# Row sums of the softmax and a one-row mask in a chain of four cross-attention layers

## Time and profile before

| what | value |
|---|---|
| median of 3 runs | 991.19 us (991.05 to 992.46) |
| profiled execution, its own time | 991.19 us |
| its span | 989.4 us |
| TensorE busy | 953.5 us (96%) |
| VectorE busy | 737.7 us (75%) |
| ScalarE busy | 574.4 us (58%) |
| GpSimd busy | 360.8 us (36%) |
| chain that ended last, TensorE's share | 80% |
| chain that ended last, VectorE's share | 8% |

### The profile page before, as it was taken

One profiled execution on the slowest core, in us unless ns is written; L12 is line 12 of the kernel. 1 busy time (PEld: TensorE's weight loads), 2 busy tenths in 40 slices (PEclk: granted clock), 3 DMA queues, 4 the chain that ended last, 5 costly groups with the idle time before them and its releaser, 6 DMA issues.

```text
span 989.4 us, 20036 instructions
## 1 busy us (share of the span) xinstructions
PE 953.5 (96%) x8028; PEld 822.3 (83%) x8028; DVE 737.7 (75%) x1259; ACT 574.4 (58%) x1193; POOL 360.8 (36%) x413
## 2 busy tenths in 40 slices
PE   6999999999998998999999999999999999999997
PEld 5777566556776998998999999999999999889997
DVE  5878999899999788565776677877666766786542
ACT  3557788787876654364545455444544554465552
POOL 2332689898641333011212222431122212282210
PEclk9999999999999999999999999999999999999999
DMA  8302000000000500034233224331222121200001
GB/s 307 106 2 86 1 2 1 2 1 1 2 1 1 204 31 2 1 130 146 74 100 107 84 96 163 108 102 48 86 87 78 51 86 46 83 1 12 23 22 33
DMA packets 31268, 62.30 MB, mean 63 GB/s; under 512 B 4420, under 2 KB 9288, under 8 KB 30536
## 3 DMA queue, kind: packets, MB, share of 16 engines
q1 hardware_dynamic: 31176, 61.02, 18.0%
HBM read 58.91 MB, written 2.10 MB: 62 GB/s over the span
## 4 chain that ended last, share of the span: by engine, by line
PE 80%; DVE 8%; ACT 4%; POOL 4%; issue 4%; DMA 0%; POOLq 0%; DVEq 0%; ACTq 0%
PE work L947 11%; PE work L801 7%; PE work L803 6%; PE work L802 6%; PE work L1060 6%; PE scores L801 6%; PE scores L803 6%; PE scores L802 6%; PE work L1024 5%; PE work L722 3%; PE work L656 3%; PE work L1042 3%; PE work L780 2%; PE work L764 2%; PE work L545 2%
## 5 line engine op out<-in xcount | busy, mean ns | idle before, releaser
L1632 DVE TENSOR_REDUCE smax<-scores 128x16 f32<-128x1024 f32 x32 | 39.2, 1224 | 110.9 <-PE scores L803 110.9
L2179 POOL TENSOR_SCALAR stat<-stat 128x2 f32<-128x2 f32 (+2 forms) x50 | 12.0, 240 | 287.1 <-DVE stat L1206 285.8
L947 PE MATMUL work<-ctxT,w 128*128 128x128 f32 x960 | 112.6, 275 | 0.2 <-DVE all_values L1617 0.2
L947 PEld LDWEIGHTS work<-ctxT,w 128*128 128x128 f32 x960 | 109.9, 192 | 0.8 <-issue 0.8
L2356 POOL TENSOR_TENSOR probs<-probs,smax 128x1024 f32<-128x1024 f32 x22 | 42.2, 1918 | 115.6 <-DVE smax L1657 115.6
L2043 ACT ACTIVATE all_keys<-work 128x512 fp32r<-128x512 f32 x64 | 38.2, 598 | 76.2 <-PE work L1024 76.2
L801 PE MATMUL work<-all_values,pT_l_high 128*128 128x256 f32 x256 | 74.9, 293 | 1.2 <-DVE pT_l_low L1625 1.2
L801 PE MATMUL scores<-all_keys,src_l_high 128*128 128x256 f32 x256 | 74.1, 290 | 0.0
L803 PE MATMUL work<-all_values,pT_l_low 128*128 128x256 f32 x256 | 71.7, 280 | 0.0
L803 PE MATMUL scores<-all_keys,src_l_low 128*128 128x256 f32 x256 | 71.7, 280 | 0.0
L802 PE MATMUL work<-all_values,pT_l_high 128*128 128x256 f32 x256 | 71.6, 280 | 0.0
(11 more groups left out here) (213 smaller groups left out, 3048.1 us busy)
## 6 DMA issues: line engine op xcount, KB each, us to landing
w<-in_l_wk SPq DMA_DIRECT2D x32, 512.0 KB, 4.1
w<-in_l_wv SPq DMA_DIRECT2D x32, 512.0 KB, 5.0
w<-in_l_wq SPq DMA_DIRECT2D x8, 512.0 KB, 5.6
w<-in_l_wo SPq DMA_DIRECT2D x8, 512.0 KB, 5.9
x<-in_x SPq DMA_DIRECT2D x1, 2048.0 KB, 14.5
pair<-in_l_wo SPq DMA_DIRECT2D x4, 512.0 KB, 3.3
out<-x SPq DMA_DIRECT2D x8, 256.0 KB, 2.1
pair<-in_xT SPq DMA_DIRECT2D x1, 1536.0 KB, 8.7
```

What stands on the lines that cost most here:

```text
L947: last = mm(bank[:, h * P:(h + 1) * P], w[:, c, h * K3:(h + 1) * K3], ctxT[:, c, p * P:(p + 1) * P], start=(c == 0), stop=(c == DC - 1))
L1632: v.tensor_reduce(m, s3, X, ALU.max).then_inc(d_lmax, 1)
```

## The change

The sums of layer 0's odd tiles and of layer 2's even tiles now go by way of GpSimd. In GpSimd's list the quarters of a unit's even tile come last in each turn of layer 2, except in turn 16, where they follow the spreading of the reciprocals. Those of layer 0's odd tiles come first in the next turn. On VectorE, turns 1 to 7 take the sum and the reciprocals behind `unit_residual` instead of ahead of it. The mask row is now held once per half of the array (partitions 0 and 64) and read by products over 64 rows (K = 64); `mask_row` is zeroed by two fills, and the row is loaded by two transfers and converted one partition at a time.

```diff
 def at_once(k):
-    return k >= FIRST[2 * B] or k < FIRST[B] and k % 2 == 1
+    return k >= FIRST[2 * B] and k % 2 == 1
...
             load("head16", head_of_row[16], A["head16"])
-            e.wait_ge(p_const, 4)
-            load("mask", mask_u8[0:P:32, :], A["mask"].broadcast_to([4, CTX]))
+            load("mask", mask_u8[0:1, :], A["mask"])
+            load("mask", mask_u8[S:S + 1, :], A["mask"])
...
-                e.wait_ge(d_mask, 2)
-                e.wait_ge(p_const, 4)
+                e.wait_ge(d_mask, 4)
+                e.wait_ge(p_const, 5)
                 for t in range(2):
                     for j in range(2):
-                        at = slice(j * S + 32 * t, j * S + 32 * t + 32)
+                        at = slice(j * S, (j + 1) * S)
                         mm(sc[t][:, j * BANK:(j + 1) * BANK], ones_bf[at, :],
-                           mask_row[f"l{layer}"][at, b * S:(b + 1) * S].unsqueeze(1).broadcast_to([32, 8, S]),
+                           mask_row[f"l{layer}"][at, b * S:(b + 1) * S].unsqueeze(1).broadcast_to([S, 8, S]),
...
-            v.tensor_scalar(mask_row["l2"][:, :], mask_u8[:, :], -1.0, -LOWEST, ALU.add, ALU.mult).then_inc(d_mask, 1)
-            e.wait_ge(d_mask, 1)
-            v.tensor_scalar(mask_row["l0"][:, :], mask_row["l2"][:, :], -LOWEST, None, ALU.mult).then_inc(d_mask, 1)
+            for i, row_of in enumerate((slice(0, 1), slice(S, S + 1))):
+                v.tensor_scalar(mask_row["l2"][row_of, :], mask_u8[row_of, :], -1.0, -LOWEST, ALU.add,
+                                ALU.mult).then_inc(d_mask, 1)
+            e.wait_ge(d_mask, 2)
+            for row_of in (slice(0, 1), slice(S, S + 1)):
+                v.tensor_scalar(mask_row["l0"][row_of, :], mask_row["l2"][row_of, :], -LOWEST, None,
+                                ALU.mult).then_inc(d_mask, 1)
...
-                if 0 < u < B or 2 * B < u <= NU:
+                if 2 * B < u <= NU:
                     tile_sums(late[0])
                     unit_reciprocals(u - 1)
...
-                if u == 2 * B:
+                if late and u <= 2 * B:
                     tile_sums(late[0])
                 if len(late) == 2:
                     tile_max(*tiles[1])
                     tile_sums(late[1])
-                if u == 2 * B:
+                if 0 < u <= 2 * B:
                     unit_reciprocals(u - 1)
...
-            g.memset(mask_u8[:, :], 1).then_inc(p_const, 1)
+            for name in ("l0", "l2"):
+                g.memset(mask_row[name][:, :], 0.0).then_inc(p_const, 1)
...
                     reciprocals_spread(u - 1)
+                if u == 2 * B:
+                    tile_sums(tiles[0][0])
...
-                if tiles and not at_once(tiles[0][0]):
+                if tiles and u != 2 * B:
                     tile_sums(tiles[0][0])
```

More of the change, by code:

```diff
@@ L774, in output @@
                     e.wait_ge(d_part, 9)
-                    e.wait_ge(p_const, 5)
+                    e.wait_ge(p_const, 6)
                     mm(work[2][:, :], ones_bf[0:96, :], bias_parts[0:96, :].unsqueeze(1).broadcast_to([96, TT, D]),
@@ L1231, in vector @@
             ln_stats("ctx", ctx_raw[:, 1:, :], CN - 1)
-            e.wait_ge(p_const, 4)
-            e.wait_ge(s_in["mask"], 16)
-            v.tensor_scalar(mask_row["l2"][:, :], mask_u8[:, :], -1.0, -LOWEST, ALU.add, ALU.mult).then_inc(d_mask, 1)
-            e.wait_ge(d_mask, 1)
-            v.tensor_scalar(mask_row["l0"][:, :], mask_row["l2"][:, :], -LOWEST, None, ALU.mult).then_inc(d_mask, 1)
+            e.wait_ge(s_in["mask"], 32)
+            e.wait_ge(p_const, 5)
+            for i, row_of in enumerate((slice(0, 1), slice(S, S + 1))):
[5 more added lines that the diff above has]
+                                ALU.mult).then_inc(d_mask, 1)
             ln_finish("ctx", ctx_raw[:, 1:, :], ctx_norm[:, 1:, :], CN - 1)
```

## The result

| | before | after |
|---|---|---|
| median | 991.83 us (991.05 to 992.50, 4 runs) | 997.52 us (996.93 to 998.47, 4 runs) |
| profiled execution, its span | 989.4 us | 995.7 us |
| TensorE busy | 953.5 us | 959.0 us |
| VectorE busy | 737.7 us | 729.8 us |
| GpSimd busy | 360.8 us | 393.6 us |

The ratio is 1.0064 [1.0051, 1.0077]: the change makes the kernel slower by 5.7 us of median; the two profiled spans are 6.3 us apart. VectorE has 7.9 us less to do and the kernel is later all the same. Lines before 1200 stand one or two lines earlier in the new file, most later ones one line later: L684 is L682, L703 is L701, L738 is L736, L1273 is L1274, L1303 is L1304, L2179 is L2180, L2213 is L2214, L2223 is L2224 and L2226 is L2227.

A forecast was written before the change was run, and what follows sets the result against it. TensorE was taken to bound layer 0, with VectorE and GpSimd both tight in layer 2. Terms 2.6 (mask), 0.3 (layer 0's odd tiles) and 5.3 (layer 2) add 8.2 us to 991.19: 999.4 us, range 994.5 to 1003.0.

The forecast's parts named there:

- The mask, 0.44 a unit: TensorE's mask products and scores: second round of 0.23 plus change of shape, 0.44 us a unit, 2.6 us in units 2 to 7.
- The upper bound of 0.49: Most a unit's mask could cost: a whole 0.39 us instruction for the second round, plus 0.12, with rounding.
- Layer 0's odd tiles, 0.3 in all: L738 waits 0.27 us for reciprocals in unit 3, not 4, and is covered from unit 5: 0.3 us, bounds 0 and 1.4.
- VectorE's order, the start, layer 1, nothing each: VectorE's new order in layer 0, extra mask loading at the start, and layer 1's turn 8 each cost 0 us.
- Turns 16 and 17, S18 3.35 late: Layer 2: GpSimd's full list delays turn 17's sum; S18, start of unit 18's first maximum on VectorE, is 3.35 us late.
- Turns 18 and 19, +0.6 and +1.6: Layer 2: GpSimd's quarters come at S + 8.43, after VectorE's place S + 6.12; unit 19 loses 0.6 us, unit 20 1.6.
- Turn 20 +0.4, and 0.2 back from S20 to S23: Layer 2: turn 20's quarters, done at S + 7.3, cost 0.4 us; then TensorE bounds, so only 0.2 us returns by unit 23.
- The sum: Mask in layer 0 2.6, layer 0's odd tiles 0.3, layer 2 5.3: 8.2 us on 991.19, giving 999.4 us.
- GpSimd is in time: Rival: GpSimd's list has room, S of units 18 to 20 doesn't slip, the masks alone cost: 995.7 us; chance 0.16.
- VectorE's relief decides: Rival: layer 2's quarters come in time and the mask's second round hides: 2.4 us gained, 988.8 us; faster: 0.06.
- The waits feed one another: Rival: L738 waits in units 3 to 7, units 20 to 22 don't recover: 10.7 us, 12 with contention, 1002 to 1003; chance 0.15.
- The change of shape is free: Rival: on TensorE a mask costs only 0.23 us, 2.5 us less, 997 us; no chance of its own given.

The follow-up runs named there:

- e1: Kernel before with only the mask over 64 rows (loads, fills, conversion, products): 994.66 us against 991.44, ratio 1.0043.
- e2: Kernel before with each of a unit's four mask products issued twice in the same 32-row shape: 992.57 us against 991.44, ratio 1.0018.
- e9: Kernel before with layer 0's odd tiles by way of GpSimd and VectorE's new order, but tile 13 summed at once: 992.07 us against 991.39, ratio 1.0016.
- e3: Kernel before with only layer 0's odd tiles by way of GpSimd and VectorE's new order, old mask: 992.98 us against 991.44, ratio 1.0016.
- e8: Changed kernel with VectorE's old order in turns 1 to 7: 998.18 us, ratio 1.0070 to the kernel before (992.26).
- e4: Kernel before with only layer 2's even tiles by way of GpSimd, in its new list places, old mask: 994.17 us against 991.44, ratio 1.0033.
- e6: Kernel before with only tiles 58 and 60 (turns 21 and 22) by way of GpSimd: 990.51 us against 992.26, ratio 0.9988.
- e7: Changed kernel with the old 32-row mask: 997.01 us, ratio 1.0051 to the kernel before (992.26).

## Why the prediction was right, and by how much it was off

The forecast was 999.4 us; it measured 997.52, inside the range. Direction and cause are as forecast. The steps, one by one:

- **The mask, 0.44 a unit:** measured 0.42, in the two forecast halves: a round of 0.21 (forecast 0.23) and a change of shape of 0.21 (forecast 0.21), shown by e1 against e2. Six units give 2.5 us (forecast 2.6). (The upper bound of 0.49 was added up wrongly: 0.39 + 0.12 is 0.51.)
- **Layer 0's odd tiles, 0.3 in all:** The wait stands in turn 3 (0.26, forecast 0.27) and not in turn 4, as forecast, and costs 0.33. But "from unit 5 on the next layer's keys and sources stand ahead of L738 and cover it" failed in turn 7: there L736 waits 0.49 us, and the unit loses some 0.5. e9 against e3 shows the cause: bias casts and subtractions that I had not counted, because they were not touched. Layer 0 as a whole is 3.3 us late (forecast 2.9). That e3 loses 0.4 in each of three turns while the changed kernel loses 0.3 once there was not foreseen either: the mask's delay is absorbed by the wait. Alone they cost 2.4 and 2.0 by unit 16; together 3.3.
- **VectorE's order, the start, layer 1, nothing each:** the order is confirmed by e8. The transposes of turn 7 are 3.32 us late and the masks of unit 16 are 3.26, so layer 1 adds nothing; the start is within 0.03.
- **Turns 16 and 17, S18 3.35 late:** measured 5.88 - 3.32 = 2.6. The place is right (3.19 us of idle, "some 3 to 4"), the size 0.8 too high. The norm starts 258.76 - 254.59 = 4.17 us later than before, 0.85 behind the delay of S16, where I had 1.34: 0.9 for turn 16's quarters, which is right, and 0.44 for the mask. The mask's share is not on the path, as e4 shows: without the mask its norm of turn 17 is 0.85 us late too and its S18 2.6. That is some 0.5 of the 0.8; the rest is 0.1 to 0.2 each, in the norm with the quarters (258.76 to 262.48 is 3.7, forecast 3.9) and in what follows the sum (262.48 to 264.87 is 2.4, forecast 2.55).
- **Turns 18 and 19, +0.6 and +1.6:** measured +0.4 and +1.4. VectorE gets its sum at S + 8.42 and S + 8.44 (forecast 8.5), and waits 2.2 and 2.3 us for it, a little over the "1 to 2" of the forecast. (The 5.1 us of list ahead of the norm should have been 0.61 + 6.00 - 1.6 = 5.0.)
- **Turn 20 +0.4, and 0.2 back from S20 to S23:** measured +0.25, and 7.71 - 7.59 = 0.1 back. The three periods take 318.96 - 287.72 = 31.2 us, as forecast. That TensorE bounds there is seen after: VectorE's maximum of unit 23 waits 0.55 us for scores. Without the mask the same quarters give 0.75 us back by unit 23, as e6 shows.
- **The sum:** layer 2 costs 7.59 - 3.32 = 4.3 us where 5.3 was forecast, layer 0 3.3 where it was 2.9. The two errors go opposite ways, so that the sum is nearer than its terms: with the last L736 it is 7.8 us against 8.2.

Of the rivals, "GpSimd is in time" falls by the waits after: it would have had no wait for quarters. "VectorE's relief decides" falls with e1, as the mask's second round is not hidden. "The waits feed one another" was right on one count (the changed GpSimd work slows VectorE's in turn 7) and wrong on the size. "The change of shape is free" falls with e2 against e1. Its price of 2.5 us was not worked out; e1 and e2 are 4.2 - 2.0 = 2.2 us apart at unit 23.

What is left is 7.8 us in the trace against 5.7 in the medians. That is no step of the forecast. The profiled executions of before and after both have one stretch of 3.4 us at the lower clock, but before has it where TensorE is full, and it costs 1.5 us there; that takes the 7.8 to 6.3, the difference of the spans. So of the 1.9 us between forecast and measured time 1.5 come from the clock, which the forecast didn't consider. The time lies within the range with them or without.

The parts don't add up, and it is worth seeing why. At S20 they cost 4.1 (mask), 2.0 (layer 0) and 4.4 us (layer 2) alone, 10.5 in all, and 7.7 together. In layer 0 the mask moves TensorE's demand for the reciprocals to where they are nearly ready. So the mask adds 1.2 us by unit 16 (3.3 after against 2.1 in e7) and not 2.4. In layer 2 GpSimd's lateness hides the mask: from S16 to S20 the changed kernel loses 7.71 - 3.32 = 4.4 us, e4 without the mask 4.4, e7 without it 4.45, and e1 with nothing else 1.6.

## What to carry to other kernels

Moving part of a reduction to an idle engine shortens the busy engine, but puts a chain of three operations in the place of one; before that is done, find the place of the new work in the helper's list and what stands ahead of it. Where its input is ready early, put it ahead of the list's late items: here that alone took back 3.3 of 4.4 us. And look on the relieved engine for any operation that will run beside the helper's new one, as its duration may not survive.

## What the runs showed of the hardware

**An addition on GpSimd holds up some of VectorE's operations until it ends.** These are single instructions in the profile after and the profile before (duration ns min/median/max, first and last start).

```profile
L1350 DVE TENSOR_TENSOR bias_rest<-pair,bias_parts x2: 415/918/1421, 87.5 to 88.0; 1x256 f32<-1x256 f32 x2
```
```profile
L1349 DVE TENSOR_TENSOR bias_rest<-pair,bias_parts x2: 415/417/419, 85.1 to 85.5; 1x256 f32<-1x256 f32 x2
```

One of the two is untouched; the other starts at 88.0, shortly after GpSimd's 1.27 us addition (from 87.83 on), and takes 1.0 us longer, about what that addition has left. In the same way one of three casts of the bias at 77 us takes 1258 ns instead of 283, beside GpSimd's addition that starts at 77.39. It is small work on one partition, and still held up. VectorE's reductions over 256 floats keep their mean of 410 ns (408 before). The Trainium skill says it in SBUF — State Buffer, section "SBUF: two separate sides": VectorE and GpSimd share a pair of ports, which is an exclusive lock, held for the whole instruction, against VectorE's operations with two SBUF inputs (where GpSimd's reads SBUF, as these additions do) or in a two-port mode. The trace agrees, with 1.0 us for one subtraction of two SBUF inputs, and that rule would have warned of turn 7. Which mode the casts ran in no run here shows.

**The granted clock of TensorE falls to half for some 3.4 us at a time.** Stretches by time of the profile before, then after (window, length, PE, PEld, DVE, ACT, POOL, PEclk, DMA share, GB/s):

```profile
397.00:400.00 3.00, 1.24 (x11) 1.05 (x10) 3.00 (x3) 0.91 (x2) 2.37 (x1) 1.00 0.00 0
400.00:401.20 1.20, 1.18 (x10) 1.20 (x11) 1.20 (x3) 0.00 (x0) 0.00 (x0) 1.00 0.00 0
401.40:404.60 3.20, 3.20 (x18) 3.20 (x17) 2.40 (x5) 1.99 (x4) 0.00 (x0) 0.51 0.00 0
405.00:407.00 2.00, 2.00 (x19) 2.00 (x19) 0.34 (x1) 0.00 (x0) 0.00 (x0) 1.00 0.00 0
```
```profile
405.00:407.00 2.00, 1.08 (x10) 0.87 (x8) 2.00 (x2) 0.75 (x2) 2.00 (x1) 1.00 0.00 0
409.00:412.00 3.00, 3.00 (x27) 3.00 (x26) 2.20 (x5) 2.00 (x4) 0.00 (x0) 1.00 0.00 0
```

Between 401.4 and 404.6 us the granted clock before is 0.51, the lower of the two levels (1.2 GHz), and the products follow one another every 0.21 us instead of every 0.12. TensorE had stood still for 1.78 us until 400.02 and then run full for 1.4 us. The delay of after against before is 7.8 us ahead of this stretch and 6.3 behind it. In the profile after the same pause lies at about 406 to 408 us and the clock behind it stays at 1.00; it has its own low stretch at 323 us, right behind a pause of 2.07 us, where it costs little: the delay is 7.6 us ahead of it and 7.8 behind. The traces of e2, e3 and e9 have a stretch near 981 us and none at 400. Of two alike pauses one is followed by a low stretch and one is not, so the pause by itself doesn't decide it. I have not tried what does.

Each such stretch costs some 1.5 us where TensorE is full, and it explains levels in the runs of one kernel. Runs whose mean clock is 1.000 took 988.34 to 989.03 us before (median 988.7, 10 runs) and 996.75 and 996.93 after, 8.2 us apart. Most runs of before (51 of 67) lie at 991.1 to 993.0, with mean clocks of 0.996 to 0.998, while of 31 runs recorded after 25 lie at 996.8 to 998.5, most of them about 1 us above their lowest, and six near 1000.2 (mean clock 0.995). So a part of what the change costs is hidden in the medians, by luck of where the stretches fall. The same comparison puts e1 at +4.7, e4 at +4.1 and, with one run each, e3 at +3.0, e9 at +2.5, e8 at +8.0 and e6 at -0.2 us. That is 0.3 to 1.1 above the delay of S23 in their traces, and this rest is open. That the 8.2 of the change is the forecast's own sum is chance too, as the trace gives 7.8 and the terms were off by more.
